# Graph attention on one core: the probabilities of a head pair mixed with V in one run of eight key tiles

## The reference

```python
q = _heads(seq_inputs @ Wq + bq)
k = _heads(seq_inputs @ Wk + bk)
v = _heads(seq_inputs @ Wv + bv)
scores = jnp.einsum('bhqd,bhkd->bhqk', q, k) / np.sqrt(HEAD_SIZE)
bias = jnp.where(graph_mask, 0.0, NEG)[:, None]
probs = jax.nn.softmax(scores + bias, axis=-1)
ctx = jnp.einsum('bhqk,bhkd->bhqd', probs, v)
ctx = ctx.transpose(0, 2, 1, 3).reshape(seq_inputs.shape[0], seq_inputs.shape[1], H)
return ctx @ Wf + bf
...
x = _layernorm(x + _L0_gnn_ref(x, ...), axis=-1)
```

## Time and profile before

| | us |
|---|---|
| median of 3 runs | 1620.8 (1620.15 to 1623.42) |
| span of the profiled execution | 1678.4 |
| TensorE matmul busy in it | 1557.5 |
| TensorE weight load | 1236.2 |
| VectorE | 1111.9 |
| ScalarE | 896.1 |
| GpSimd | 345.4 |

### The profile page before, as it was taken

How to read it: one execution, slowest core, us unless ns; L and a number is a source line. 1 busy time by engine, 2 the same in 40 slices (tenths; PEclk the granted TensorE clock), 3 DMA queues, 4 the chain that set the end, 5 groups by cost and what they waited for, 6 DMA issues and landing times.

```text
span 1678.4 us, 30828 instructions
## 1 busy us (share of the span) xinstructions
PE 1557.5 (93%) x10320; PEld 1236.2 (74%) x10320; DVE 1111.9 (66%) x2044; ACT 896.1 (53%) x1605; POOL 345.4 (21%) x656
## 2 busy tenths in 40 slices
PE   7989989999899998999898998999989998999994
PEld 6867778677777777777686776877768676787773
DVE  6667657676667666677565775767756676577672
ACT  5556545565355544556445564466644565446561
POOL 1222022221222211222112221122211222112111
PEclk9999999999999999999999999999999999999997
DMA  4112112121122211212112121122210321112210
GB/s 135 43 43 59 32 43 70 30 45 33 43 70 36 45 27 43 70 40 53 26 31 73 34 50 32 31 73 45 45 33 24 78 47 39 34 31 36 45 32 25
DMA packets 110893, 76.47 MB, mean 46 GB/s; under 512 B 59776, under 2 KB 98432, under 8 KB 110720
## 3 DMA queue, kind: packets, MB, share of 16 engines
q1 hardware_dynamic: 110720, 74.29, 18.3%
HBM read 36.31 MB, written 12.78 MB: 29 GB/s over the span
## 4 chain that ended last, share of the span: by engine, by line
PE 41%; DMA 32%; issue 14%; SPq 5%; DVE 4%; POOL 2%; ACT 1%; POOLq 0%; DVEq 0%; ACTq 0%
DMA spread_dram<-inv_sum 24%; PE turn_ps L448 9%; PE score_ps L438 9%; PE context_ps L463 8%; DMA inv_rows<-spread_dram 5%; PE misc_ps L371 4%; PE misc_ps L373 4%; PE misc_ps L372 4%; DMA q_swap<-q_home 3%; SPq L328 3%; PE score_ps L371 1%; PE score_ps L372 1%; PE score_ps L373 1%; SPq L281 1%; DVE prob L608 1%
## 5 line engine op out<-in xcount | busy, mean ns | idle before, releaser
L608 DVE CUSTOM_DVE_ANT_0 prob<-score_ps,mask 128x1024 f32<-128x1024 f32 x384 | 468.3, 1221 | 65.1 <-PE score_ps L438 57.7
L541 ACT ACTIVATE prob<-prob,row_min 128x1024 f32<-128x1024 f32 x384 | 439.7, 1145 | 57.4 <-DVE row_min L608 52.0
L534 ACT ACTIVATE prob_t<-turn_ps 128x512 f32<-128x512 f32 x384 | 229.4, 597 | 396.4 <-PE turn_ps L448 388.9
L448 PE MATMUL turn_ps<-ident,prob 128*128 128x128 f32 x3072 | 413.9, 277 | 4.8 <-DVE prob_t L617 3.7
L463 PE MATMUL context_ps<-prob_t,v_all 128*64 128x256 f32 x3072 | 380.4, 392 | 33.3 <-DVE context L628 33.3
L448 PEld LDWEIGHTS turn_ps<-ident,prob 128*128 128x128 f32 x3072 | 343.4, 141 | 85.8 <-issue 64.3
L617 DVE COPY prob_t<-turn_ps 128x512 f32<-128x512 f32 x384 | 264.9, 690 | 180.8 <-PE turn_ps L448 177.9
L463 PEld LDWEIGHTS context_ps<-prob_t,v_all 128*64 128x64 f32 x3072 | 207.7, 139 | 179.7 <-issue 60.2
L728 POOL TENSOR_TENSOR context_lo<-context,context_hi 128x256 fp32r<-128x256 f32 x96 | 70.5, 734 | 1122.3 <-ACT context_hi L552 1122.3
L438 PE MATMUL score_ps<-k_stack,q_home 128*128 128x512 f32 x768 | 270.2, 433 | 11.6 <-DMA q_swap<-q_home 10.5
L438 PE MATMUL score_ps<-k_stack,q_swap 128*128 128x512 f32 x768 | 241.5, 396 | 0.0
(11 more groups left out here) (59 smaller groups left out, 1805.5 us busy)
## 6 DMA issues: line engine op xcount, KB each, us to landing
q_swap<-q_home SPq DMA_DIRECT2D x192, 128.0 KB
x_in<-in_x_dram SPq DMA_DIRECT2D x32, 384.0 KB, 6.0
inv_rows<-spread_dram SPq DMA_DIRECT2D x192, 64.0 KB, 3.9
out_dram<-res SPq DMA_DIRECT2D x32, 384.0 KB, 3.0
adj_in<-in_adj_dram SPq DMA_DIRECT2D x64, 128.0 KB, 3.6
spread_dram<-inv_sum SPq DMA_DIRECT2D x96, 2.0 KB
prob_t<-in_L_gnn_Wk_dram SPq DMA_DIRECT2D x1, 576.0 KB, 4.0
prob_t<-in_L_gnn_Wq_dram SPq DMA_DIRECT2D x1, 576.0 KB, 7.2
```

The costliest lines, as they stand in the source:

```text
L448: last = pe.transpose(turn_ps[:, half, i, :], prob[:, u % 3, kt * P:(kt + 1) * P], ident[:])
L534: nc.scalar.activation(prob_t[:, pair % 2, head, 0:4, qt * P:(qt + 1) * P], turn_ps[:, 0], ACT.Copy).then_inc(copied[0], 1)
L541: nc.scalar.activation(prob[:, t % 3, :], prob[:, t % 3, :], ACT.Exp, scale=-1.0, bias=row_min[:, t % 4:t % 4 + 1], accum_out=row_sum[:, t ...
L608: nc.vector.tensor_tensor_reduce(prob[:, t % 3, :], score_ps[:, t % 2, :], mask[:, qt, :], 1.0, HUGE, ALU.add, ALU.min, row_min[:, t % 4:t ...
```

## The change

The two mixing runs of a pair become one run over all eight key tiles. It stands in unit 4p + 8, a multiple of four, between where the two stood. In the tail the first run of pair 10, which stood in unit 47, joins the second. Everything else keeps its place in the list; the body of the mix step, its waits and its semaphores are the same.

```diff
-        if t >= 7 and t % 2 == 1:
-            steps.append(("mix", (t - 7) // 4, (t - 7) % 4 // 2))
+        if t >= 8 and t % 4 == 0:
+            steps += [("mix", t // 4 - 2, 0), ("mix", t // 4 - 2, 1)]
...
-    steps += [("turn", units - 2), ("mix", last - 1, 1), ("turn", units - 1), ("denominators", last)]
+    steps += [("turn", units - 2), ("mix", last - 1, 0), ("mix", last - 1, 1), ("turn", units - 1), ("denominators", last)]
```

## The result

| | before | after |
|---|---|---|
| median | 1620.5 us (1610.7 to 1623.4, 4 runs) | 1668.9 us (1666.5 to 1681.5, 4 runs) |
| ratio | | 1.0335 (95% interval 1.0283 to 1.0387) |
| profiled execution, time / span | | 1666.5 / 1664.6 us |

The change costs 48 us. I had said 58, and 1679 for the time. In the runs that give both, an execution's time is its span plus 2 us. So the first profile of before, with its span of 1678.4, had caught an execution some 58 us longer than the median, and its rows must be compared with care. Experiment e1 profiled the same kernel again and caught an ordinary one (span 1612.5).

The account below looks back on a forecast made before the run. PE's own work was taken to bound the kernel. With 29 us gained by fewer shape changes and 87 lost to stalls, +58 on 1620.8 gave 1679 us, range 1640 to 1713.

Parts of the forecast that it names:

- Fewer shape changes: PE, two four-tile mixing runs joined: 0.33 us gained per pair, 29 us in all, called certain as PE time.
- The wait on the product before: First half of a mix, three units behind the context product in place of two: PE waits less; gain taken as 0.
- The cover that goes: Transposes without mixing ahead wait for VectorE's copy: stall 0.82 us, net +0.49 per q pair, +2.5 per batch.
- The projections: Second projection tile in a pair's third unit (units 22, 34): stall 1.46 us, net +1.13 each, +2.3 per batch.
- The x tiles and the end: Units 38 and 39, 41 to 43, 45 to last x tile: bank and copy waits, +0.4, +0.57, +1.74, sum +2.7.
- Which time it is added to: Base of the forecast: unprofiled median 1620.8 us, taken as nearly free of the profile's overlong distances; gives 1679 us.
- Rival A: Transposes' second half in a pair's fourth unit: stalls don't come, faster, 1592 us; chance 0.08 in full or in part.
- the sign of being right: In the waits view, transposes held by VectorE's copy at 50 to 90 us.
- Rival B: Denominators' DMA round trip ahead of the context product becomes the bound: +32 us, 1711 us; chance 0.09.
- Rival C: PE's clock falls after stalls; if at each of the 80, over 200 us more; chance 0.01.

Follow-up runs that it names:

- e9: Changed kernel with each pair's one long mixing run in unit 4p + 7 in place of 4p + 8: 1685.1 us against 1669.7, ratio 1.0079.
- e2: Changed kernel with, on VectorE alone, a q piece or projection behind its unit's copy in place of ahead of it: 1673.2 us, ratio 1.0365.
- e4: Changed kernel with the q pieces of units 10, 14, 18, 26 and 30 one unit later: 1668.3 us, ratio 1.0331.
- e3: Kernel before with the same VectorE edit as e2, the copy ahead of q piece or projection: 1622.4 us, ratio 1.0044.
- e6: Changed kernel with the four x loads of unit 12 spread over units 15, 19, 23 and 27: ratio 1.0256.
- e7: Kernel before with the four x loads of unit 12 spread over units 15, 19, 23 and 27: ratio 0.9910.
- groups 2 to 4: Runs e5 to e8, e9 to e11, and e12, each group on another chip; there the kernel before had medians of 1642.0, 1669.7 and 1640.5 us.
- e11: e10 with the x loads also spread over units 15, 19, 23 and 27: 1640.5 us, ratio 0.9853 to the kernel before.
- e5: Changed kernel with e2's copy-first order only in the third units of pairs up to unit 34: 1676.4 us against 1642.0, ratio 1.0122.
- e8: Changed kernel with the edits of e5 and e6 together: median 1668.6 us, ratio 1.0125 to the kernel before.
- e10: e9 with the q pieces of units 24 and 36 moved to units 23 and 35: 1668.4 us, ratio 0.9989 to the kernel before.
- e12: Changed kernel with the edits of e4 and e6 together: 1672.2 us against 1640.5, ratio 1.0169.

## Why the prediction was right

The direction, the mechanism and the order of size were right. Step by step:

*Fewer shape changes, 0.33 per pair.* The run of x32 takes 3.67 us, as in the earlier trace rows, and PE is busy 5.3 us less than in e1. The gain by itself shows where nothing else changed: 12.33 to 12.05 in e9, 0.28. Slightly less than said.

*The wait on the product before, taken as 0.* 2.6 us once, where e1 had 17.9 in six waits. In a quiet pair 0 was right. But 14.7 of the 17.9 lay in five waits at units 17 to 21, where the kernel after has none, and that place is shorter in the mean (-1.15): a gain that I had put at nothing. e9 shows what it becomes with the run one unit earlier than I had it here.

*The cover that goes.* The chain came out within 0.02 us up to the transposes behind the piece of q. Predicted from the start of the transposes: scores 0.85, minimum 2.26, copy 3.41, context product 4.09, transposes 4.72. Measured: 0.85, 2.25, 3.40, 4.09, 4.74. Further on it slips a little: the first half of the last transposes at 6.68 where I had 6.51, the second at 7.70 where I had 7.73. The pair takes 12.82 where I said 12.82. That it is VectorE's order is shown by e2 (12.21 with the copy first), that it is the place of the job by e4 (12.11), and that the cover matters by e3 (no effect where the short runs stand between).

*The projections.* 1.13 said, 0.98 measured, twice.

*The x tiles and the end: the term that was mis-sized.* "0.4", "0.57" and "+1.74", a sum of 2.7; measured 0.10, 0.30 and 1.12, a sum of 1.5. With 1.2 us too much per batch, seven times, that is 8 of the 10 us by which the forecast was high. Each of the three stretches is some 0.4 too high. For units 38 and 39 the rows show why, first e1, then after:

```profile
365.19 0.62 PE L438 MATMUL score_ps<-k_stack,q_swap 128*128 128x512 f32 x2
366.08 0.55 PE L391 MATMUL misc_ps<-ident,x_in 128*128 128x128 f32 x3 [0.26 <-DVE q_home L591]
...
371.23 0.63 PE L438 MATMUL score_ps<-k_stack,q_swap 128*128 128x512 f32 x2
372.15 0.55 PE L391 MATMUL misc_ps<-ident,x_in 128*128 128x128 f32 x3 [0.29 <-DVE q_home L591]
```

The first x tile starts 0.89 us behind the scores in e1 and 0.92 after, where 0.47 is usual. I had priced that wait for the bank at 0.7 as new, and the kernel before had it already; what is new is 0.26 at the tile behind it. In units 41 to 44 the new waits are 0.38 and 0.10, where I had 0.6 and 0.3, and at the end 0.95 and 1.0, where I had 1.1 and 1.3. Why these are smaller than the chains gave is not shown.

*What I left out:* by the shortest distances the place of unit 8 (+0.14) and 0.4 more in that of units 17 to 21, against 0.5 less in the tail; together nothing, but the last rests on one pass of eight, as said above. By the means what I left out is the late swap at units 25 to 29 (+1.4 beyond the 0.49) and late denominators, which go either way. That the sum came so close to the medians is luck in this part.

*Which time it is added to.* The level was right, for a simpler reason than I gave. The unprofiled runs were not "nearly free" of late DMAs: e1 has 71.3 us of idle time ahead of the context product and its x-load place is 3 us longer in the mean than at its shortest. The first profile had simply caught a long execution.

*Rival A* (1592) fell: the waits it needed under 20 us are 39.3 on the matmuls. Of the 50 to 90 us that I had named as the sign of being right, the weight loads show 55.2 and the matmuls fall short with 39.3. The rule of the Trainium skill beside it (page TensorEngine Tiling (Array Packing), section Key Properties: changing the tiling mode drains TensorE) agrees with the 0.28 us per pair that halving the switches gave in e9. *Rival B* fell as the cause of the loss in the quiet pairs; in the one shown the product waits for nothing (78.59, right behind the reciprocal). In all, the idle time ahead of the product went down, not up, and e6 against e7 loses the same. But its idea, that the time between pairs is bounded by a round trip over DRAM and SyncE's queue, is what limits the cures: e2 and e4 show it. *Rival C* fell: the granted clock is 0.987 in after and in e1, so stalls of 0.8 us do not lower it.

*What stays open.* The late swaps of q. In the kernel after they are issued some 8 us ahead of the scores that need them and were late in one batch of eight. The waits for them in the other traces (us, times): before, first profile, 10.5 us in 5; e1 and e11 none; e2 0.6 in 1; e4 0.3 in 1; e5 20.9 in 6; e6 14.2 in 4; e7 2.7 in 2; e8 29.0 in 7; e9 4.7 in 1; e10 4.0 in 1; e12 18.0 in 4. The spread loads alone don't explain that, since e5 has the loads where they were, in unit 12; nor does the changed order alone, since the first profile of before has such waits and e4 all but none. No run moved one load alone, each changed kernel was profiled once, and e5 and e8 were profiled in their longest execution, so the cause stays open. How much of what e5 still loses is such waits isn't known either. And e11 was not run beside e7, nor the change itself on the chips of groups 2 to 4.

## What to carry to other kernels

A stretch of matmul work that needs no one is not only cost: it is cover for whatever another engine must empty in the meantime. Before joining two such stretches, list the PSUM banks with a single buffer that were emptied behind each, and write out the chain of the emptying engine for the units left bare; here a saved 0.3 us met a stall of 0.8. Then choose the place of the long run so that the unit with the most work for the emptying engine has it behind it.

Before a local stall is removed, ask what the pair behind it waits for. e2, e4 and e12 did in the quiet pairs just what they should, and most of it was given back: in e2 at late denominators and at the jobs that had had cover, in e4 at late denominators, in e12 at late swaps. And when a job is moved, look at every queue that it takes something along in: in e4 it was a swap ahead of the very write that the next pair waited for.

## What the runs showed of the hardware

- The same kernel had medians of 1614, 1642, 1670 and 1640 us on four chips. The differences looked for here are of the same size, so a kernel without its own runs of before beside it would have told nothing.
- During a wait of 6.62 us on PE the granted clock fell to 0.50, the level of 1.2 GHz, and was back at 1.00, 2.4 GHz, six us after the work had resumed, a mean of 0.63 over its first 8 us. The long run in it took 5.60 us in place of 3.67, and the pair was 9.7 us longer than the shortest at its place. Stalls of 0.4 to 1.1 us, 65 of them, left the mean clock at 0.987, that of e1.
- A denominators' write of 2 KB to DRAM, issued at 82.27, let its read back start only at 93.00, 10.7 us later, beside the x loads; for the pairs that write later in that batch it was 8.0 to 9.0 us.
